# Transposes of the normalised rows of a two-layer ranking network: from the second layer into the first

## What is computed

```python
cont_emb = emb_table[:13][None] * conts[:, :, None]
cate_emb = emb_table[cates]                       # 26 gathered rows for each sample
cc = concatenate([cont_emb, cate_emb], axis=1)    # 39 fields of 64
pairs = einsum('bfd,bgd->bfg', cc, cc)[:, ROWS, COLS]
X = concatenate([cont part, cate part, pairs], axis=1)
X = relu(layernorm(X @ W1 + b1, ln1_g, ln1_b))    # 1024 wide
X = relu(layernorm(X @ W2 + b2, ln2_g, ln2_b))    # 1024 wide
logit = sigmoid(X @ Wout + bout)
```

## Time and profile before

| what | value |
|---|---|
| median of 3 runs | 777.32 us (774.78 to 778.52) |
| the profiled execution, its time | 778.39 us |
| its span, first to last instruction | 776.9 us |
| TensorE busy | 731.6 us, 94% of the span |
| VectorE, ScalarE, GpSimd busy | 582.2, 516.1, 481.3 us |
| granted TensorE clock, mean | 0.979 |

### The profile page before, as it was taken

How to read it: one execution, slowest core, us unless ns; L and a number is a source line. 1 busy time by engine, 2 the same in 40 slices (tenths; PEclk the granted TensorE clock), 3 DMA queues, 4 the chain that set the end, 5 groups by cost and what they waited for, 6 DMA issues and landing times.

```text
span 776.9 us, 11960 instructions
## 1 busy us (share of the span) xinstructions
PE 731.6 (94%) x3583; PEld 596.8 (77%) x3583; DVE 582.2 (75%) x1735; ACT 516.1 (66%) x978; POOL 481.3 (62%) x450
## 2 busy tenths in 40 slices
PE   5598899999999999999999999999999999999995
PEld 1356778888888888778788877878878888888884
DVE  7357977878878888787787877878787566565568
ACT  3487877868778687686867868677665535545441
POOL 6777877777777777777777777777000433434431
PEclk9798979999999999999999999999999999999998
DMA  8961111111111111111111111112463111101000
GB/s 323 347 228 25 23 54 28 54 54 26 54 39 40 52 25 52 34 45 52 25 54 25 52 54 26 52 25 59 176 216 124 55 29 54 54 27 54 27 1 0
DMA packets 26644, 53.37 MB, mean 69 GB/s; under 512 B 11024, under 2 KB 11351, under 8 KB 26554
## 3 DMA queue, kind: packets, MB, share of 16 engines
q1 hardware_dynamic: 10570, 31.29, 12.0%
q0 software_dynamic: 13312, 13.06, 7.3%
q10 hardware_dynamic: 2736, 8.71, 2.8%
HBM read 45.20 MB, written 11.63 MB: 73 GB/s over the span
## 4 chain that ended last, share of the span: by engine, by line
PE 44%; POOL 30%; issue 17%; DVE 4%; DMA 2%; ACT 2%; POOLq 0%; ACTq 0%; DVEq 0%
POOL xb L513 27%; PE acc L546 13%; PE acc L548 13%; PE acc L547 13%; POOL xb L510 3%; PE gr L612 1%; PE tr L612 1%; DMA xb<-in_L_rec_emb_table,idx_all 1%; PE gr L714 1%; PE tr L714 1%; DMA xb<-table_scratch,idx_all 1%; PE tr L570 0%; PE gr L570 0%; DMA last_row<-in_L_rec_emb_table 0%; ACT dots L830 0%
## 5 line engine op out<-in xcount | busy, mean ns | idle before, releaser
L513 POOL DMA_INDIRECT xb<-table_scratch,idx_all x390 | 381.3, 978 | 118.9 <-issue 116.4
L546 PE MATMUL acc<-w_hi,x_hl 128*128 128x512 f32 x416 | 172.9, 416 | 4.5 <-DVE x_hl L1115 3.1
L548 PE MATMUL acc<-w_hi,x_hl 128*128 128x512 f32 x416 | 165.5, 398 | 0.0
L547 PE MATMUL acc<-w_lo,x_hl 128*128 128x512 f32 x416 | 165.0, 397 | 0.0
L530 POOL TENSOR_TENSOR raw_lo<-raw_lo,raw_hi 128x1024 f32<-128x1024 f32 x14 | 33.5, 2391 | 146.8 <-ACT raw_lo L998 146.8
L546 PE MATMUL acc<-w_hi 128*128 128x512 f32 x256 | 100.9, 394 | 0.0
L548 PE MATMUL acc<-w_hi,w_lo 128*128 128x512 f32 x256 | 99.7, 389 | 0.0
L547 PE MATMUL acc<-w_lo,w_hi 128*128 128x512 f32 x256 | 99.7, 389 | 0.0
L794 ACT CAST g_still<-x_hl 64x384 fp32r<-64x384 f32 (+1 forms) x128 | 97.9, 765 | 2.5
L546 PEld LDWEIGHTS acc<-w_hi,x_hl 128*128 128x128 f32 x416 | 80.0, 192 | 20.8 <-issue 4.1
L548 PEld LDWEIGHTS acc<-w_hi,x_hl 128*128 128x128 f32 x416 | 79.7, 192 | 18.5
(11 more groups left out here) (121 smaller groups left out, 1313.3 us busy)
## 6 DMA issues: line engine op xcount, KB each, us to landing
raw_lo<-in_L_rec_W SPq DMA_DIRECT2D x26, 512.0 KB, 5.4
h_scratch<-h_row ACTq DMA_DIRECT2D x16, 512.0 KB, 2.9
raw_hi<-h_scratch SPq DMA_DIRECT2D x16, 512.0 KB, 3.5
xb<-table_scratch,idx_all POOLq DMA_INDIRECT x390, 2.4
table_scratch<-in_L_rec_emb_table SPq DMA_DIRECT2D x4, 781.2 KB, 7.9
raw_hi<-in_L_rec_W SPq DMA_DIRECT2D x6, 512.0 KB, 5.7
raw_hi<-in_L_rec_b SPq DMA_DIRECT2D x1, 512.0 KB, 4.3
raw_hi<-in_L_rec_ln_g SPq DMA_DIRECT2D x1, 512.0 KB, 5.2
```

The source lines that it names most:

```text
L513: done = nc.gpsimd.indirect_dma_start(out=to, out_offset=None, in_=table, in_offset=at_row)
L546: nc.tensor.matmul(o, a, w, start=first, stop=False)
L547: nc.tensor.matmul(o, a, v, start=False, stop=False)
L548: return nc.tensor.matmul(o, b, w, start=False, stop=last)
```

## The change

The eight transposes of a tile's normalised rows are made in layer 1. In iteration x, between "gram 1" and "gram 2" (behind k tile 7), TensorE turns `h1_row` of tile x-1 into `acc[1 - par]`, whose sums have been normalised by then. ScalarE and VectorE copy one half each back to `h1_row`, and the store takes it turned. In layer 2 `transpose2` is gone, and `relu1` reads the loaded rows from SBUF. The last tile is turned within `product2(0)`, behind its k tile 4. On VectorE `turn_dots` moves from the end of an iteration to the start of the next, behind `split_group(x, 0)`, and `cate_pairs` and `split_group(x, 1)` change places. The second and the last tile's programs are changed alike.

```diff
-          "gram 0", 6, "gram 1", 7, "gram 2", 8, "gram 3", 9, 10, "next 0", 11, 12)
+          "gram 0", 6, "gram 1", 7, "turn prev", "gram 2", 8, "gram 3", 9, 10, "next 0", 11, 12)
...
@@ SyncE: load_h1
-                eng.wait_ge(t2_ready, x - 1)
+                eng.wait_ge(y_ready, K2 * (x - 1))
...
@@ TensorE
+            def turn_h1(x, par):
+
+                pe.wait_ge(norm_act, x + 1)
+                pe.wait_ge(norm_dve, x + 1)
+                for k in range(K2):
+                    last = nc.tensor.transpose(acc[par][:, k // 4, (k % 4) * P:(k % 4 + 1) * P],
+                                               h1_row[:, k * P:(k + 1) * P], ident[:, :])
+                last.then_inc(h1_turned, 1)
...
@@ iteration
-                    pe.wait_ge(norm_act, x - 1)
-                    pe.wait_ge(norm_dve, x - 1)
+                    pe.wait_ge(h1t_act, x - 1)
+                    pe.wait_ge(h1t_dve, x - 1)
...
@@ last iteration, and product2
-                            transpose2(0, 0)
...
-                    if k == 0:
-                        transpose2(x + 1, 1 - par)
+                    if first and k == K2 // 2:
+                        turn_h1(TILES - 1, 1)
...
@@ ScalarE
+            def turned_h1(x, par):
+
+                act.wait_ge(h1_turned, x + 1)
+                nc.scalar.copy(h1_row[:, 0:HALF], acc[par][:, 0, :]).then_inc(h1t_act, 1)
+                h1_store(x)
...
                 norm1(x - 1, 1 - par, rooted=True)
-                h1_store(x - 1)
-                for q in range(1, FILLS):
+                take_dots(x, 1)
+                turned_h1(x - 1, 1 - par)
+                for q in range(2, FILLS):
                     take_dots(x, q)
...
@@ ScalarE: relu1
-                act.wait_ge(t2_ready, x + 1)
+                act.wait_ge(h1_in[par], 8 * x + 16 - 8 * par)
...
@@ VectorE
+            def turned_h1(x, par):
+
+                dve.wait_ge(h1_turned, x + 1)
+                nc.vector.tensor_copy(h1_row[:, HALF:HID], acc[par][:, 1, :]).then_inc(h1t_dve, 1)
...
             def iteration(x, par, last=False):
 
+                turn_dots(x - 1)
                 cate_features(x - 1)
                 still_low(x, 0)
+                split_group(x, 1)
                 cate_pairs(x - 1)
-                split_group(x, 1)
                 still_low(x, 1)
                 factor_lo(x - 1)
...
                 norm1(x - 1, 1 - par, lambda: take_dots(x, 0))
-                for q in range(1, FILLS):
+                take_dots(x, 1)
+                turned_h1(x - 1, 1 - par)
+                for q in range(2, FILLS):
                     take_dots(x, q)
                 if last:
                     last_features(x)
                 else:
-                    turn_dots(x)
                     split_group(x + 1, 0)
```

More of the change, by code:

```diff
@@ L95 @@
 SECOND = (0, 1, 2, 3, "factor prev", "own 1", "late prev", 13, 4, 14, 5, 15, 6, "own 2", 16, 17, 18, 7, "own 3", 8, 9,
-          "gram 0", "gram 1", 10, "gram 2", "gram 3", 11, "next 0", 12)
+          "gram 0", "gram 1", 10, "turn prev", "gram 2", "gram 3", 11, "next 0", 12)
 LAST = (0, "own 1", 1, 2, 3, "factor prev", 4, "own 2", "late prev", 13, 14, 15, "own 3", 16, 17, 18, 5,
-        "gram 0", 6, "gram 1", 7, "gram 2", 8, "gram 3", 9, 10, 11, "factor", 12)
+        "gram 0", 6, "gram 1", 7, "turn prev", "gram 2", 8, "gram 3", 9, 10, 11, "factor", 12)
 EMB_WAIT = {a: g + 1 for g, (a, b) in enumerate(GROUPS)}
@@ L285, in build @@
         norm_dve = sem("norm_dve")
+        h1t_act = sem("h1t_act")
+        h1t_dve = sem("h1t_dve")
         h1_out = sem("h1_out")
@@ L292, in build @@
         h1_in = [sem("h1_in0"), sem("h1_in1")]
-        t2_ready = sem("t2_ready")
+        h1_turned = sem("h1_turned")
         y_ready = sem("y_ready")
@@ L638, in _, with share @@
             transpose_group(0, 0, first=True)
-            def share(x, what, first, last):
+            def turn_h1(x, par):
[5 more added lines that the diff above has]
+                last.then_inc(h1_turned, 1)
+            def share(x, par, what, first, last):
                 if what == "own 1":
@@ L659, in share @@
                     late(x - 1)
+                elif what == "turn prev":
+                    turn_h1(x - 1, 1 - par)
             def k_tile(x, par, kt):
@@ L683, in iteration @@
                     if isinstance(what, str):
-                        share(x, what, first, last)
+                        share(x, par, what, first, last)
                     elif what < EK:
@@ L703, in iteration @@
                     product2(0, 0, first=True)
[L705 to L716, removed]
             def product2(x, par, first=False, last=False):
                 if isinstance(x, int) and x < 2:
-                    pe.wait_ge(norm_act, TILES - 1 + x)
-                    pe.wait_ge(norm_dve, TILES - 1 + x)
+                    pe.wait_ge(h1t_act, TILES - 1 + x)
+                    pe.wait_ge(h1t_dve, TILES - 1 + x)
                 else:
@@ L771, in h1_store @@
             def h1_store(x):
-                act.wait_ge(norm_act, x + 1)
-                act.wait_ge(norm_dve, x + 1)
+                act.wait_ge(h1t_act, x + 1)
+                act.wait_ge(h1t_dve, x + 1)
                 stands_alone(act)
@@ L931, in second_tile @@
                 norm1(0, 0)
-                h1_store(0)
-                for q in range(FILLS):
+                for q in range(2):
+                    take_dots(1, q)
+                turned_h1(0, 0)
+                for q in range(2, FILLS):
                     take_dots(1, q)
@@ L971, in relu1 @@
             def relu1(x, par):
-                t = tr if par == 0 else gr
-                act.wait_ge(t2_ready, x + 1)
+                act.wait_ge(h1_in[par], 8 * x + 16 - 8 * par)
                 if not isinstance(x, int) or x >= 1:
@@ L977, in relu1 @@
                 for k in range(K2):
-                    nc.scalar.activation(y[:, k, :], t[:, k // 4, (k % 4) * P:(k % 4 + 1) * P], ACT.Relu,
+                    nc.scalar.activation(y[:, k, :], h1[par][:, k * P:(k + 1) * P], ACT.Relu,
                                          bias=be1_col[:, k:k + 1], scale=g1_col[:, k:k + 1]).then_inc(y_ready, 1)
@@ L1007, in _ @@
             norm1(TILES - 1, 1)
-            h1_store(TILES - 1)
+            turned_h1(TILES - 1, 1)
             act.wait_ge(acc_ready, TILES)
@@ L1321, in second_tile @@
                 norm1(0, 0)
-                for q in range(FILLS):
+                for q in range(2):
                     take_dots(1, q)
-                turn_dots(1)
+                turned_h1(0, 0)
+                for q in range(2, FILLS):
+                    take_dots(1, q)
                 split_group(2, 0)
             def iteration(x, par, last=False):
+                turn_dots(x - 1)
                 cate_features(x - 1)
                 still_low(x, 0)
+                split_group(x, 1)
                 cate_pairs(x - 1)
-                split_group(x, 1)
                 still_low(x, 1)
```

## The result

| | median | runs |
|---|---|---|
| before | 777.46 us | 4, 774.78 to 778.52 |
| changed | 790.07 us | 4, 789.70 to 790.72 |

The ratio is 1.0172, 95% interval 1.0151 to 1.0194: the changed kernel is 1.7% slower. The forecast was 796.3, range 786 to 802. The profiled execution took 789.84 us with a span of 788.0, against 778.39 and 776.9 before. So 11.45 us have to be found between these two traces, where the forecast had 19.0.

What follows compares the result with a forecast made beforehand. TensorE was taken to bound both layers, held by gathers late in layer 1. Terms -1.2 - 8.4 + 18.2 + 2.4 + 4.6 + 3.4 = +19.0 gave 797.4, or 796.3 us on the median's scale, range 786 to 802.

Steps and rivals of the forecast that it cites:

- The bound: Both layers: TensorE sets the pace, 31.98 us a tile in layer 1, held from tile 8 by GpSimd's gathers at 33.1.
- VectorE's order: Layer 1: `turn_dots` delays `factor_lo`, so TensorE waits 1.3 us at k tile 13 in 14 tiles: +18.2 us.
- The transposes: Both layers: sixteen blocks leave layer 2, 13.9 us saved; fifteen come in layer 1, one in `product2(0)`, 12.7: net -1.2 us.
- the wait for `norm1`: Layer 1, at the new block ahead of "gram 2": 0.17 us a tile in 14 tiles, +2.4 us (0 to 5).
- The cushion: Layer 1: TensorE's waits for gathers absorb added work, all used up: -8.4 us.
- The handover: In `product2(0)`: the last tile's block waits for `norm1(15)`, +4.6 us (3.9 to 4.8).
- The clock: In `product2(0)`: the long wait there lowers TensorE's clock once, 6.8 us at the lower level, +3.4 us (0 to 5).
- rival D: Layer 1: the clock falls in every tile, 3.4 us each, about 845; with a few such tiles 801 to 815; chance 0.08 shared.
- main case: Whole kernel: the summed terms hold, 791 to 801 us; chance 0.70.
- rival C: Layer 1, k tile 13: half the stall, 0.5 to 0.9 us a tile, 785 to 791 us; chance 0.10.
- A: Layer 1: `factor_lo` and `norm1` in time, clock unmoved, the gathers pay: -5.0, 772.3 us; chance 0.07.
- B: Layer 1: `factor_lo` in time, but norm wait, handover and clock as forecast: +0.8, 778.1 us, no change; chance 0.05.

Runs made afterwards that it cites:

- e3b: The kernel before with only VectorE's new order (`turn_dots` at the next iteration's start, `cate_pairs` and `split_group(x, 1)` exchanged): 784.72 us, ratio 1.0097.
- e7: The kernel before with eight dummy transposes of the identity a tile in layer 1, ahead of "gram 2", layer 2 keeping its own: 782.19 us, ratio 1.0067.
- e1b: The changed kernel with `turn_dots` put back to the end of the iteration: 774.69 us, ratio 0.9964 to the kernel before.
- e2b: The changed kernel with `factor_lo` moved ahead of `still_low(x, 1)` on VectorE, `turn_dots` left in its new place: 773.87 us, ratio 0.9952 to the kernel before.
- e6: e5 with the block of transposes behind "gram 2" instead of ahead of it: 772.34 us, ratio 0.9943 to the kernel before.
- e5: The changed kernel with `turn_dots` back at the iteration's end and the last tile turned behind k tile 7 of `product2(0)`: 770.65 us, ratio 0.9919 to before.
- e4b: The changed kernel with the last tile turned behind k tile 7 of `product2(0)` instead of k tile 4: 785.43 us, ratio 1.0114 to the kernel before.
- e1: The changed kernel with `turn_dots` back at the iteration's end, on a slower chip: 999.53 us, 1.0425 of the kernel before there.

## Why the prediction was right, and where its sizes were off

**The bound.** TensorE at 31.98 us a tile, the gathers at 33.1 behind it: e3b and e7 show both, since what was added to TensorE arrived only in part. (GpSimd did wait for TensorE at times in the kernel before, 2.1 us in seven pieces, where the prediction read "none for anybody". It changes no term.)

**VectorE's order, the term that decided.** Place and mechanism as forecast, and shown by e1b and e2b from both sides. Forecast 1.3 a tile and 18.2 in all; measured 33.99 - 32.95 = 1.04 and 14.6, both under the ranges given for them (1.1 to 1.6, 15 to 22). The sum over VectorE's rows was good: `factor_lo` was to end at +12.50 and ended at +12.31 to +12.59, on average +12.42, in the tiles from 3 on. What was mis-sized was mainly the 0.2 added for semaphore and weight load: TensorE began 0.06 behind `factor_lo`'s end. That is 0.14 of the 0.26 a tile, and the earlier end of `factor_lo` another 0.08.

**The transposes and the wait for `norm1`.** Forecast 0.79 + 0.17 = 0.96 a tile in layer 1, measured 0.97 in e1b and 0.98 in e7. By e6 the 0.95 of e5 divide into 0.83 for the block and 0.12 for the wait, where the forecast had 0.79 and 0.17. In layer 2, 0.87 forecast and 0.89 measured.

**The cushion.** 8.4 forecast, 8.6 in e3b; the waits of "own 3" are gone.

**The handover.** 4.6 forecast, 4.10 measured: `norm1(15)` ended 11.0 us behind the start of `product2(0)`, at 608.99, where the forecast had 11.3. That it is this wait, and that it moves to the copies, e4b shows.

**The clock.** One spell, behind the 4.1 us wait, as forecast. It was 3.4 us long where the forecast put 6.8, and cost 1.6 instead of 3.4: the block took 1.60 us instead of 0.79, and the next four matmuls another 0.8. The length was luck, though. In e2b the same wait, 4.13 us, was followed by

```profile
590.00:597.00 7.00, 3.16 (x12) 2.89 (x13) 4.23 (x13) 3.27 (x8) 0.00 (x0) 0.65 0.27 77
597.00:604.00 7.00, 7.00 (x28) 5.65 (x27) 2.75 (x6) 3.77 (x11) 0.00 (x0) 0.86 0.19 75
```

that is (0.35 + 0.14) x 2 x 7 = 6.9 us at the lower level, the forecast's length. The block and the eight matmuls behind it took 2.5 us longer there; part of the spell fell into the wait itself, which the forecast's half of 6.8 did not allow for. In e1b, behind 4.11 us, the spell was 3.4 us again. The early pair of waits from which the 6.8 had been read the earlier trace rows led to 3.4 us only in e1b, 0.12 x 2 x 14, behind waits of 1.67 and 1.37 us. So one trace does not give the length of a spell, and by these runs the term lies at 1.6 or 2.5. The steady waits of up to 1.02 us left the clock at 1.00, and rival D falls.

The Trainium skill, "TensorE: Matmul & The Clock Gate", section "Part 4: PE-mode transpose", says that transposes don't count as activity for the gate. Layer 1 from 125 to 550 us, with thirteen blocks in it, is at 1.00 in the changed kernel and in e1b, so the rule, true or not, costs nothing here; whether it holds, no run here shows.

**The sum.** From measured sizes: 15 x 0.97 in layer 1, 0.8 for the last block (what it took longer is in the clock's term), less 16 x 0.89 in layer 2: +1.1. With +14.6 for the order, -8.4, +4.1 and +1.6 this is +13.0; the traces differ by 11.45. The missing 1.6 lie in the main before tile 3: "next 0" of tile 2 is at 108.40 instead of 109.30, although a block had been added ahead of it, and the clock from 100 to 112 us was 0.86 instead of 0.59. All seven kernels with a block ahead of "gram 2" or behind it in tile 1 read 0.81 to 1.00 there, the two without 0.59. So it goes with the block; by what, no run here shows. The forecast was 7.6 too high: 3.6 by the order's term, 1.8 by the clock, 0.5 by the handover, 0.1 by the transposes, 1.6 by the early spell.

All these errors point the same way, and their sum carried the time out of the main case, 791 to 801, and into the band of rival C, 785 to 791, which stood for a stall of 0.5 to 0.9 us a tile. C isn't what happened: the stall is 1.04. The time alone could not have told them apart; the spacing of "next 0" does.

Rivals A and B stood for `factor_lo` in time, and e1b and e2b make that true. e1b keeps the handover, the clock's spell and the wait for `norm1`, so it is B's kernel. B had 778.1, no change; e1b took 774.69, 0.4% under before, 3.4 us under B, about the size of the clock's 1.8 and the early spell's 1.6. A, 772.3, left out the clock's loss and the wait for `norm1`. Its statement that the gathers pay for all holds for layer 1: 32.95 us a tile is no more than the 33.08 that the gathers take.

## What to carry to other kernels

An engine that is idle 17% of the time can still have a stretch with no slack in it: before work is moved on such an engine, find the wait that ends each stretch (here the one for the transposes of "next 0") and add up what stands between it and the next thing that the bound engine needs. Moving work from behind that release into idle time ahead of it, or the needed result forward in the queue, repaired the same wait, 1.0 to 1.1 us a tile. And where a second resource holds the bound engine back a little in each round, price added work against that cushion first, and spend it once.

## What was not expected of the hardware

The whole program ran 23% longer on one chip than on the others, 959.49 against 777 us, with waits of TensorE between two matmuls of one group (64.4 us in 58 pieces in e1) that the profile puts down to nothing. A comparison between kernels from that chip would have read the cure e1 as 4% slower than before, where elsewhere it is 0.4% faster.

With a block of eight transposes in tile 1 the clock from 100 to 112 us was 0.81 to 1.00 in seven kernels, against 0.59 in the two without.

And nearly equal holes brought TensorE's clock down for unequal times: 3.4 us behind holes of 4.10 and 4.11 us, 6.9 us behind one of 4.13; 6.8 us behind 1.68 and 1.36 us close together, 3.4 us behind 1.67 and 1.37. Holes of 0.7 to 1.2 us once in every 34 us did not bring it down.
